# The turned form of the state update in the first five steps of a gated-linear-attention and mixture-of-experts kernel

## The reference

```python
q = (x @ Wq).reshape(B, S, H, DK)              # H = 8 heads, DK = 128
k = (x @ Wk).reshape(B, S, H, DK) * DK ** (-0.5)
v = (x @ Wv).reshape(B, S, H, DV)              # DV = 64
alpha = jax.nn.sigmoid((x @ Wg + bg) / GATE_NORM)
def step(state, inp):
    qt, kt, vt, at = inp
    state = at[..., None, None] * state + kt[..., None] * vt[:, :, None, :]
    out_t = jnp.einsum('bhk,bhkv->bhv', qt, state)
    return (state, out_t)
...
return out * jax.nn.sigmoid(x @ Wog) @ Wo
```

## Time and profile before

| | |
|---|---|
| median of 3 runs | 1276.55 us (1276.54 to 1277.82) |
| the profiled execution | 1277.6 us, of which the span of instructions is 1275.8 |
| mean granted TensorE clock | 0.998 |
| PE busy | 1253.5 us, 98% |
| DVE busy | 935.7 us, 73% |
| ACT busy | 575.7 us, 45% |
| steps 0 to 4 | from about 16 to 390 us of the span |

### The profile page before, as it was taken

One profiled execution on the slowest core, in us unless ns is written; L12 is line 12 of the kernel. 1 busy time (PEld: TensorE's weight loads), 2 busy tenths in 40 slices (PEclk: granted clock), 3 DMA queues, 4 the chain that ended last, 5 costly groups with the idle time before them and its releaser, 6 DMA issues.

```text
span 1275.8 us, 27850 instructions
## 1 busy us (share of the span) xinstructions
PE 1253.5 (98%) x9702; PEld 1108.0 (87%) x9702; DVE 935.7 (73%) x2215; ACT 575.7 (45%) x1171; POOL 486.1 (38%) x377
## 2 busy tenths in 40 slices
PE   7999999999999999999999999999999999999999
PEld 6788888888888888898898888988988899889887
DVE  6997878889797559867578586675785866757834
ACT  6565655656564444433344333333443343334422
POOL 2110011011001016437557375474574754745620
PEclk9999999999999999999999999999999999999999
DMA  6567535355342322257487475674874756747665
GB/s 237 166 234 216 174 108 169 121 174 170 121 153 76 101 78 89 88 137 189 109 191 172 120 170 132 160 189 103 188 171 118 170 135 156 188 106 186 157 194 185
DMA packets 124918, 194.66 MB, mean 153 GB/s; under 512 B 12016, under 2 KB 98608, under 8 KB 124592
## 3 DMA queue, kind: packets, MB, share of 16 engines
q1 hardware_dynamic: 94384, 147.99, 35.9%
q0 software_dynamic: 30464, 45.83, 19.9%
HBM read 148.62 MB, written 57.74 MB: 162 GB/s over the span
## 4 chain that ended last, share of the span: by engine, by line
PE 84%; DVE 11%; issue 2%; DMA 1%; ACT 1%; DVEq 0%; SPq 0%; ACTq 0%
PE bank L785 24%; PE bank L837 7%; PE bank L942 7%; PE bank L910 7%; PE bank L800 7%; PE bank L817 6%; PE bank L952 4%; PE bank L855 4%; PE bank L858 4%; PE bank L828 3%; PE bank L882 3%; PE bank L932 2%; DVE Dt L1485 2%; PE bank L894 2%; PE bank L870 2%
## 5 line engine op out<-in xcount | busy, mean ns | idle before, releaser
L627 POOL DMA_INDIRECT acc<-arena,idx_all x128 | 215.1, 1681 | 141.8 <-issue 74.5
L619 POOL DMA_INDIRECT arena<-table,idx_all x132 | 170.5, 1292 | 167.5 <-ACT share L1162 113.5
L785 PE MATMUL bank<-xp,wq 128*128 128x512 f32 x768 | 214.9, 415 | 0.0
L785 PE MATMUL bank<-xp,wk 128*128 128x512 f32 x768 | 202.3, 398 | 0.2 <-DVE wk L1395 0.2
L785 PEld LDWEIGHTS bank<-xp,wk 128*128 128x128 f32 x768 | 141.8, 188 | 34.0 <-DVE wk L1395 0.6
L785 PEld LDWEIGHTS bank<-xp,wq 128*128 128x128 f32 x768 | 141.0, 190 | 28.0 <-issue 0.5
L1485 DVE TENSOR_TENSOR_SCAN Dt<-decay,eye_b 128x512 f32<-128x512 f32 x128 | 157.2, 1230 | 0.0
L837 PE MATMUL bank<-qT,kT 128*128 128x128 f32 x1024 | 135.5, 275 | 1.8 <-DVE At L1506 1.8
L1138 ACT ACTIVATE qT<-bank 128x512 f32<-128x512 f32 x128 | 76.5, 598 | 130.9 <-PE bank L785 128.8
L837 PEld LDWEIGHTS bank<-qT,kT 128*128 128x128 f32 x1024 | 125.1, 192 | 2.7 <-DVE At L1506 2.1
L1138 ACT ACTIVATE kT<-bank 128x512 f32<-128x512 f32 x128 | 76.4, 597 | 99.1 <-PE bank L785 98.6
(11 more groups left out here) (172 smaller groups left out, 2235.8 us busy)
## 6 DMA issues: line engine op xcount, KB each, us to landing
decay<-decay_dram SPq DMA_DIRECT2D x64, 512.0 KB, 5.1
carry<-decay_dram SPq DMA_DIRECT2D x60, 512.0 KB
arena<-in_L_attn_x_dram SPq DMA_DIRECT2D x16, 512.0 KB, 4.6
table<-arena SPq DMA_DIRECT2D x16, 512.0 KB, 3.7
xT_dram<-arena SPq DMA_DIRECT2D x16, 512.0 KB, 3.0
arena<-in_L_ffn_w_gate_dram SPq DMA_DIRECT2D x64, 128.0 KB
arena<-in_L_ffn_w_up_dram SPq DMA_DIRECT2D x64, 128.0 KB
arena<-in_L_ffn_w_down_dram SPq DMA_DIRECT2D x64, 128.0 KB, 3.8
```

The costliest lines, as they stand in the source:

```text
L619: pool.indirect_dma_start(out=xg[:, e % 2, j, :], out_offset=None, in_=table[:, :], in_offset=bass.IndirectOffsetOnAxis(ap=idx_all[:, e, j ...
L627: pool.indirect_dma_start(out=acc[:, :], out_offset=bass.IndirectOffsetOnAxis(ap=idx_all[:, e, j:j + 1], axis=0), in_=yb[:, e % 2, j, :], ...
L785: last = mm(to[:, :], w[:, part, k, h * DK:(h + 1) * DK], xp[:, other, k, :], start=(k + i == 0), stop=(k == KD - 1 and i == 2))
```

## The change

The function `turned` goes, and the turned form is used in every step but the last. In steps 0 to 4 PE therefore does nothing for the sum in odd slots; in even slots it does both heads ahead of `outputs`, and the four transposes behind it. The waits on `ut_cp` and `ut_ps` count from step 0. DVE's sum reads bank 6 in the other layout. ACT gets the copy `update_copy` in each even slot of steps 0 to 4: in slots 2 and 6 behind the keys' copy and ahead of `normalise`, in slots 4 and 8 behind `og_gate` and ahead of `sigmoids`.

```diff
-        def turned(kind):
-            return kind in ("count", "slots", "experts")
...
-            def keys_back(c, kind, h):
+            def keys_back(c, h):
                 pe.wait_ge(qk_cp, at(c, 16, 2 * h + 2))
                 if not (isinstance(c, int) and c == 0 and h == 0):
                     pe.wait_ge(kw_cp, at(c, 8, h))
-                if turned(kind) and h % 2 == 0:
-                    wait_past(pe, ut_cp, 4 * (c - S_COUNT) + h // 2)
+                if h % 2 == 0:
+                    wait_past(pe, ut_cp, at(c, 4, h // 2))
...
-            def update(c, h):
-                pe.wait_ge(kw_cp, at(c, 8, h + 1))
-                if h > 0 and h % 2 == 0:
-                    pe.wait_ge(state_up, at(c, 4, h // 2))
-                if h == 0 and not (isinstance(c, int) and c == 0):
-                    pe.wait_ge(wo_cp, 4 * c)
-                for b in range(B):
-                    lo = (h % 2) * B * DV + b * DV
-                    last = mm(bank[6][:, lo:lo + DV], kw[:, h % 2, b, :], V[:, b, h * DV:(h + 1) * DV],
-                              start=True, stop=True)
-                if h % 2:
-                    last.then_inc(u_ps, 1)
-
-            def update_turned(c, p):
+            def update(c, p):
...
             def update_back(c, p):
 
-                pe.wait_ge(ut_cp, 4 * (c - S_COUNT) + p + 1)
+                pe.wait_ge(ut_cp, at(c, 4, p) + 1)
                 if p > 0:
                     pe.wait_ge(state_up, at(c, 4, p))
-                else:
+                elif not is_first(c):
                     pe.wait_ge(wo_cp, 4 * c)
...
-                    if s % 2 == 0 and turned(kind):
-                        update_turned(c, s // 2 - 1)
+                    if s % 2 == 0 and not is_last(c):
+                        update(c, s // 2 - 1)
                     if s % 2 == 0:
                         outputs(c, s // 2 - 1)
                     beside(c, kind, s, 4)
-                    if s % 2 == 0 and turned(kind):
+                    if s % 2 == 0 and not is_last(c):
                         update_back(c, s // 2 - 1)
-                    if kind == "norm":
-                        update(c, s - 1)
                     beside(c, kind, s, 3)
...
             def update_copy(c, p):
-                act.wait_ge(ut_ps, 4 * (c - S_COUNT) + p + 1)
+                act.wait_ge(ut_ps, at(c, 4, p) + 1)
...
                     if s in (1, 4, 5, 7) and place == 2:
                         og_gate(c, kind, (1, 4, 5, 7).index(s))
+                    if s in (4, H) and place == 2:
+                        update_copy(c, s // 2 - 1)
                     if s in (1, 4, H) and place == 2:
                         sigmoids(n)
...
+                    if kind == "norm" and s in (2, 6):
+                        update_copy(c, s // 2 - 1)
                     if kind == "norm" and s % 3 == 0:
                         normalise(STEP_N * c + 1 + s // 3)
...
-            def pair_state(c, kind, p):
+            def pair_state(c, p):
 
                 both = state[:, 2 * p:2 * p + 2].rearrange("p u b v -> p (u b) v")
-                summed, added = both, bank[6][:, :].rearrange("p (r v) -> p r v", v=DV)
-                if turned(kind):
-                    summed = state[:, 2 * p:2 * p + 2]
-                    added = bank[6][:, :].rearrange("p (b u v) -> p u b v", b=B, u=2)
+                summed = state[:, 2 * p:2 * p + 2]
+                added = bank[6][:, :].rearrange("p (b u v) -> p u b v", b=B, u=2)
                 if is_first(c):
                     dve.wait_ge(u_ps, at(c, 4, p) + 1)
-                    dve.tensor_copy(both, added).then_inc(state_up, 1)
+                    dve.tensor_copy(summed, added).then_inc(state_up, 1)
                     return
```

More of the change, by code:

```diff
@@ L902, in out_proj @@
                 if isinstance(c, int) and c == C - 1:
-                    pe.wait_ge((ut_cp, state_up)[b // 2], 4 * (C - 1 - (0, S_COUNT)[b < 2]))
+                    pe.wait_ge((ut_cp, state_up)[b // 2], 4 * (C - 1))
                 elif b == 1:
@@ L1000, in step @@
                 if not is_last(c):
-                    keys_back(c, kind, 0)
+                    keys_back(c, 0)
                 scores(c, 0)
@@ L1009, in step @@
                     if s > 1 and not is_last(c):
-                        keys_back(c, kind, s - 1)
+                        keys_back(c, s - 1)
                     if s > 1 and not is_last(c):
@@ L1692, in step @@
                         if not is_last(c):
-                            pair_state(c, kind, s // 2 - 1)
+                            pair_state(c, s // 2 - 1)
                     beside(c, kind, s, 4)
```

## The result

| | before | after |
|---|---|---|
| median of 5 runs | 1276.63 us (1276.54 to 1277.82) | 1282.87 us (1282.82 to 1282.92) |
| ratio after to before, 95% interval | | 1.0045 [1.0031, 1.0059] |
| span of the profiled execution | 1275.8 | 1281.0 |
| PE, ACT busy | | 1248.0, 588.0 |

What follows compares the result with a forecast made beforehand. Early steps were taken as bound by PE for a third and by DVE for two thirds; 1.3 (step 0) + 0.8 (slot 2) - 1.3 (edges) = +0.8 on a median of 1276.55 gave 1277.4 us, range 1275.0 to 1280.0.

Steps and rivals of the forecast that it cites:

- Slot 6, steps 1 to 4: Slot 5's dropped sum (0.86) pays for the pair's sum ahead of the outputs (0.93), and DVE holds: 0.0.
- Slots 3 and 7: Odd slots 3 and 7: 0.0, since PE's lead ends at the next wait for ACT or DVE.
- slot 4 of steps 1 to 4: PE does the sum while it waited for `At`, router ready before DVE's L1306: 0.0, margin about 0.1.
- the rival of slot 4: ACT's copy makes slot 4 late in every step: 1279.6 if 0.6 later, 1284 if 1.67; chance 0.14.
- Slot 1, 0.0: Head 0's sum ahead of the router only covered its wait for ACT's token copy; removing it gives 0.0.
- Slot 2, +0.8: The pair's sum ahead of the outputs makes DVE 0.2 late, four times: +0.8 us.
- Slot 4 of step 0: Router 1.67 later behind ACT's sigmoid and copy, DVE 0.9 late, another 0.5 in slot 6: +1.3 us.
- The wait that was forecast: Sign: in slot 4 of step 0 PE idles over 1 us ahead of the transposes, released by ACT.
- Edges, -1.3: Behind slot 8's outputs 0.49 replaces 0.94; waiting for L1389 lets 0.45 through in step 1, 0.29 in steps 2 to 4.
- PE busy for some 7 us less, with a span that is not shorter: Sign in the changed kernel's whole profile: PE busy some 7 us less, span not shorter.
- The rule of the pace: The skill's 81 ns a matmul makes the new group's 16 passes 1.30, no gain; prediction expected 58 ns, 0.93.
- The strong rival: PE bounds the second part of early steps too, so its saving arrives: 5 to 7 us faster, 1270 to 1272; chance 0.07.

Runs made afterwards that it cites:

- e2: Kernel before, with only pair 1 in the turned form in steps 0 to 4: median 1279.69 us, ratio 1.0019.
- e1: Kernel before, with only pair 0 in the turned form in steps 0 to 4: median 1277.92 us, ratio 1.0008.
- e4: Kernel before, with only pair 3 in the turned form in steps 0 to 4: median 1276.01 us, ratio 0.9989.
- f1: Kernel before, with the odd slots' sums left out of steps 0 to 4, 17 us less PE work: median 1279.15 us, ratio 1.0016.
- g4: Kernel before, with ten unread products ahead of the last outputs of each of steps 0 to 4: median 1282.28 us, ratio 1.0036.
- f3: Kernel before, with four extra unread ACT copies in each of steps 0 to 4, PE's program untouched: median 1277.70 us, ratio 0.9998.
- e3: Kernel before, with only pair 2 in the turned form in steps 0 to 4: median 1283.39 us, ratio 1.0041.
- h1: Kernel before, with five unread products ahead of the last outputs of each of steps 0 to 4: median 1278.21 us, ratio 1.0004.
- g2: Kernel before, with pairs 0, 1 and 3 in the turned form in steps 0 to 4, pair 2 in the old: median 1278.89 us, ratio 1.0012.

## Why the prediction was wrong, by its own steps

**The step that failed**: "Slot 6, steps 1 to 4. The dropped sum of slot 5 (0.86) pays for the pair's sum ahead of the outputs (0.93), and DVE holds: 0.0." The 0.93 was right (224.42 to 225.35). The 0.86 was never there to be had: PE's way from the keys' projection to `keys_back` went from 2.33 to 2.42. I had made exactly this argument for slot 1, where the sum covered the tokens' copy, and didn't ask the same of slots 3, 5 and 7, where kT's copy has only this sum between the projection and its use. "Slots 3 and 7: 0.0, since PE's lead ends at the next wait" was of the same kind: behind slot 2 PE had no lead but was 0.46 late, and slot 3 gave nothing against it. Pair 2 measured +3.0 by itself and +3.7 beside the others.

**A second term, too small**: slot 4 of steps 1 to 4, where "PE does the sum in the time in which it waited for `At`". The sum is 0.93, the wait was 0.72, and PE came to it late. I had the router 0.05 to 0.1 late; with pair 1 alone it is 0.18 and DVE does not notice (steps 2 and 3 of e2 are 75.56 and 75.52, against 75.48 and 75.50), but in the changed kernel it is 0.59, L1292 at 213.79 starts 0.2 later behind the row ahead of it than L1306 did, and the 0.6 arrives in slot 6 on top of the pair's sum. So the rival of slot 4 came in by half. ACT's copy starts 20.17 behind `At` of head 1 (210.72), where I had 19.65 (208.69), and the transposes wait 0.36 for it in each of the four steps; that is near the 0.6 for which the rival had 2.0 to 2.4 us. Its reason is another, though: the sigmoid itself starts 0.52 late (210.22 after, 208.19 in the earlier trace rows), as PE's lateness from slot 2 delays the tokens that ACT copies ahead of it.

Had I asked, the rows were there for slot 5: ACT's copy of kT ended at 217.99 and `keys_back` began at 218.04, as near as the router stood to its copy in slot 1. The group was worth nothing in slot 5, `gated` of slot 6 at 224.55 stood 0.2 to 0.3 behind the outputs' end (the last four began at 223.89, 0.39 long), and 0.93 less 0.2 to 0.3, in four steps, is +2.5 to +2.9 for pair 2 where I had 0.0.

**The other terms.**
- Slot 1, 0.0: held; the router waits 0.74 for the tokens' copy in step 2, and begins 1.33 us behind the last turning of tokens in both traces.
- Slot 2, +0.8: held; e1 measured +0.6, and +0.8 in steps 1 to 4 alone; `gated` waits 0.27 in step 2 of the changed kernel.
- Slot 4 of step 0, +1.3: too small; the whole of step 0 measured +1.9. The collision held: from `gated` of slot 4 to `outs_low` it is 4.15 us (60.59 to 64.74) where it was 2.51, 1.64 more against 1.63 forecast. But there too "PE, which has dropped an odd slot's 0.86, is 0.8 late" counted on slot 5's sum; PE waits 0.69 for the keys' copy instead, and `At` of head 5 is 1.66 late where I had 0.9. That the +1.4 of e2 by itself (68.61 against 67.17) is near 1.3 is partly luck, since 0.5 of my 1.3 stood for slot 6, which e2 leaves as it was. The wait that was forecast, of more than 1 us ahead of the transposes and released by ACT, is there:

```profile
61.00 0.66 PE L878 MATMUL bank<-ident,kw 128*128 128x128 f32 x4 [1.19 <-ACT kw L1134]
```

- Edges, -1.3 (0.45 in step 1, 0.29 in the others): held; e4 measured -1.2, of it 0.5 in step 1, 0.2 in steps 2 and 3 and 0.3 in step 4. In the changed kernel this gain comes too: the projection follows the end of `xp`'s row by 0.16 in step 2 where it was 0.39, 0.2 to 0.5 less at each of the four edges. It is taken off a row that is itself 1.27 later.
- "PE busy for some 7 us less, with a span that is not shorter": 5.5 less.
- The rule of the pace: the new group's 16 passes take 0.93 (224.42 to 225.35), 58 ns each, in the norm steps as in step 5. The 81 ns of the Trainium skill, "TensorE: Matmul & The Clock Gate", section "Back-to-back issue gap", does not hold here; its section "Wait — 56ns, not 53.3ns?" gives 55.6 ns for the same moving size at full clock, and this the trace supports.

**The strong rival** (PE's saving arrives, 5 to 7 us) is refuted by f1: even 17 us taken away do not arrive.

## What to carry to other kernels

Before counting a removed group as a gain, ask of the very next instruction on that engine what it waits for and when that is ready; the removed group may have been the cover of a copy's latency, and then what it gives is only its length less the wait that appears. Do it in every place where the group stands, since here the answer was seen in one slot of four and missed in three. When a change moves work from covered places to one just ahead of the busy engine's input, its cost is the moved work less the slack that stands there (0.93 less 0.27 in slot 6). A wait can be filled once: two pieces that each fit it alone can overrun it together, as pairs 0 and 1 did in slot 4. And a change made of repeated parts is best tried part by part, as one pair here was 1.2 us better by itself (by its trace) while all four were 6.2 worse.

## What was not expected of the hardware

- f32 products with 64 columns of weights and 128 moving go at 55 to 58 ns a pass where they alternate between the two halves of a bank's partitions (outputs, the pair's sum), and at 105 ns where all go to the same half (g4's 20 passes in 2.1 us, at a granted clock of 1.00). A price read from one group doesn't hold for another with the same shapes. That the halves make the difference is not shown: g4's passes also all have the same operands and the same target.
- After a wait of 1.57 us behind dense work the granted clock fell in f3 and not, after 1.56, in the profiled execution of before; e3 fell after its waits at 160 and 314 us (1.40 and 1.39) and not after that at 238 us (1.41). Each of these falls lasted 3.4 us by the granted clock and cost 1.7 where PE had no slack. The changed kernel, with waits of at most 0.54 us at its edges, shows none in its trace, and its five runs spread over 0.1 us; but it does wait 1.8 us for `At` near 37 us, as all the kernels do, and the clock fell behind that one in before and in e3 and not in it. The Trainium skill, "TensorE: Matmul & The Clock Gate", section "HAM oscillation — how this bites in real kernels", describes a kernel whose clock falls behind its waits and whose next burst starts slow; the traces agree in kind, and add that it happens in some executions of the same kernel. That the wait is the cause is argued from these traces; h1's runs don't settle it, and g2's two groups of runs speak against it as the whole cause of the spread.
- A fall at 36 to 44 us of the kernel before (0.97 and 0.60 of full) cost nothing that shows: step 0 is 67.17 with it, and 67.16 without it in e4, whose step 0 is the same up to the last slots.
